# Window attention in a fused fp32 kernel: scores in 32-row tiles, keys staged per channel pair, TensorE's order skewed by one more unit

## The reference

```python
q = _win(roll(qs[idx], -4), 8)                      # 64 windows an image, 64 queries each
if idx == 0: k, v = _win(roll(ks[0])), _win(roll(vs[0]))     # 64 keys a window
else:        k, v = _win(roll(down(ks[1]))), _win(...)       # 2x2 stride-2 depthwise conv: 16 keys
atn = softmax(einsum('nqc,nkc->nqk', q, k) * SCALE, axis=-1)
y_  = einsum('nqk,nkc->nqc', atn, v)
```

## Time and profile before

| | |
|---|---|
| median of 3 runs | 864.39 us |
| profiled execution | 861.69 us |
| its span | 859.9 us |
| busy TensorE / VectorE / ScalarE / GpSimd | 692.2 / 719.1 / 584.7 / 603.3 us |
| mean granted TensorE clock | 0.964 |

### The profile page before, as it was taken

How to read it: one execution, slowest core, us unless ns; L and a number is a source line. 1 busy time by engine, 2 the same in 40 slices (tenths; PEclk the granted TensorE clock), 3 DMA queues, 4 the chain that set the end, 5 groups by cost and what they waited for, 6 DMA issues and landing times.

```text
span 859.9 us, 30275 instructions
## 1 busy us (share of the span) xinstructions
PE 692.2 (80%) x12282; PEld 500.2 (58%) x12282; DVE 719.1 (84%) x935; ACT 584.7 (68%) x1089; POOL 603.3 (70%) x401
## 2 busy tenths in 40 slices
PE   5968888885999958888888788888878887777763
PEld 1325565554446647666766666667666666555542
DVE  3469999997322119999999999999999999999975
ACT  2646776774213239788788798888888988777714
POOL 3047888781410008898898998999999999989960
PEclk9989999998999979999999999999999999999976
DMA  4000000000481148555555555565466555555302
GB/s 164 1 0 2 1 0 0 0 0 0 112 204 27 21 106 207 140 156 151 141 140 162 145 158 147 143 166 161 120 167 166 141 157 152 160 146 156 96 4 98
DMA packets 29937, 90.69 MB, mean 105 GB/s; under 512 B 10622, under 2 KB 10750, under 8 KB 29566
## 3 DMA queue, kind: packets, MB, share of 16 engines
q1 hardware_dynamic: 26672, 88.12, 38.3%
q10 hardware_dynamic: 3150, 0.88, 0.5%
HBM read 79.01 MB, written 3.28 MB: 96 GB/s over the span
## 4 chain that ended last, share of the span: by engine, by line
PE 40%; DVE 39%; issue 15%; ACT 2%; DMA 1%; POOL 1%; DVEq 1%; ACTq 0%; SPq 0%; POOLq 0%
PE PS L1128 40%; DVE region L767 19%; DVE region L779 9%; DVE region L645 2%; DVE region L601 2%; DVE region L605 1%; DVE region L620 1%; DVE region L607 1%; PE PS L1210 1%; DVE region L602 1%; DMA region<-px_scratch 1%; ACT region L874 0%; DVE region L575 0%; DVE region L561 0%; DMA cst<-in_consts 0%
## 5 line engine op out<-in xcount | busy, mean ns | idle before, releaser
L1128 PE MATMUL PS<-region 64*64 64x144 f32 (+3 forms) x10112 | 456.4, 292 | 112.6 <-issue 81.2
L1128 PEld LDWEIGHTS PS<-region 64*64 64x64 f32 (+1 forms) x10112 | 342.2, 134 | 219.9 <-issue 198.3
L767 DVE TENSOR_TENSOR region<-PS,region 128x864 f32<-128x864 f32 x384 | 381.2, 1046 | 12.4 <-PE PS L1128 12.3
L509 POOL TENSOR_TENSOR region<-region 128x768 f32<-128x768 f32 x128 | 202.4, 1581 | 67.5 <-DVE region L767 67.5
L513 POOL TENSOR_TENSOR region<-region 128x864 f32<-128x864 f32 x128 | 224.0, 1750 | 18.7 <-POOL region L509 0.4
L1006 ACT ACTIVATE region<-region 128x1152 f32<-128x1152 f32 x128 | 149.2, 1165 | 34.3 <-PE PS L1128 30.6
L1003 ACT ACTIVATE region<-region,cst 128x1152 f32<-128x1152 f32 x128 | 159.2, 1244 | 7.7 <-DMA region<-px_scratch 6.3
L779 DVE TENSOR_REDUCE region<-region 128x32 f32<-128x960 f32 x128 | 145.9, 1140 | 1.5 <-POOL region L513 1.5
L1037 ACT ACTIVATE region<-x,cst (+2 forms) x288 | 86.7, 414 | 0.0
L1128 PE MATMUL PS<-wg,xp 64*64 64x144 f32 x1024 | 82.6, 286 | 5.0 <-issue 4.9
L432 POOL TENSOR_TENSOR region<-region,cst 128x1024 f32<-128x1024 f32 x32 | 61.4, 1917 | 31.4 <-PE PS L1203 25.3
(11 more groups left out here) (118 smaller groups left out, 590.6 us busy)
## 6 DMA issues: line engine op xcount, KB each, us to landing
region<-px_scratch SPq DMA_DIRECT2D x256, 288.0 KB, 4.3
out<-region SPq DMA_DIRECT2D x4, 512.0 KB, 3.0
region<-xp SPq DMA_DIRECT2D x8, 140.2 KB, 2.9
region<-xp SPq DMA_DIRECT2D x8, 140.1 KB, 2.8
region<-xp SPq DMA_DIRECT2D x8, 140.0 KB, 2.9
cst<-in_consts SPq DMA_DIRECT2D x1, 1104.0 KB, 8.6
region<-xp SPq DMA_DIRECT2D x8, 132.0 KB, 2.7
region<-xp SPq DMA_DIRECT2D x8, 131.9 KB, 2.7
```

The lines of the kernel that those rows point to most:

```text
L509: pool.tensor_tensor(two_rows[:, :, :, 0:2 * THIRD - KEEP], two_rows[:, :, :, 0:2 * THIRD - KEEP], two_rows[:, :, :, KEEP:2 * THIRD], ALU. ...
L767: v.tensor_tensor(uu[:, 2 * u:2 * u + 2, :, THIRD * t:THIRD * (t + 1)], PS[:, 2 * t:2 * t + 2, 0:THIRD * C].rearrange("p h (a o) -> p h o ...
L1128: return nc.tensor.matmul(o, l, r, start=start, stop=stop)
```

## The change

- **Scores.** A product now takes 32 rows, the channels of two images (tile r, four of them), and 64 queries as weights, straight from `qw`. Its moving operand is `kb[part, i % 2, window]`: 160 columns, 64 + 64 keys of head 0 (each image of the pair masked by "e0") and 16 + 16 of head 1 ("e1"). Row tile r writes bank r, so the scores of one unit fill banks 0 to 3, and the outputs of attend move to bank 4, values and back to bank 5.
- **Staging.** ScalarE writes the masked keys, for a whole row of windows at once and one image of each pair at a time (`stage_keys`, two instructions of 512 and 128 elements, twice per row). GpSimd keeps one product per row: the halved values `vb` (1024 elements). `qs` and `vs` and their copies go away. The first keys are written between ScalarE's copies of the projections.
- **Values.** Head 0's values are picked by a product with every second group of 8 columns of the identity (four products 64x32), head 1's likewise (two products 128x64), where four transposes of 128x128 stood. ScalarE reads 64 + 128 columns of them. attend's products skip columns nobody reads (18 and 72 for 32 and 128).
- **Order.** attend and back come one unit later on TensorE, and VectorE inverts and normalises n-2 in unit n. back(n-3) also waits for `vt_out` of n-1, since it shares the bank.
- **Halving.** The last quarter (`halve(3)`) moves into units 4 to 7, one tap of both each.
- Loops are written out.

```diff
+            def stage_values(i):
+                pool.wait_ge(down_step, 8 * (i // 2 + 1))
+                if i >= 2:
+                    pool.wait_ge(vt_ready, done(4 * i - 5))
+                pool.tensor_tensor(
+                    vb[:, i % 2].rearrange("p w (b k) -> p w b k", b=B),
+                    kv4[:, WS * i:WS * (i + 1), 1, :].unsqueeze(2).to_broadcast([P, WS, B, K2]),
+                    mid(c_("h1"), WS).unsqueeze(3).to_broadcast([P, WS, B, K2]), ALU.mult).then_inc(vb_ready, 1)
+            stage_values(0)
+            for i in range(NWR):
+                if i < NWR - 1:
+                    stage_values(i + 1)
+                    pool.wait_ge(lead_step, 2 * i + 2)
+                    rows = x13[:, WS * (i + 1):WS * (i + 2), 1:W]
+                    pool.tensor_tensor(rows, rows, tap1, ALU.add).then_inc(lead_ready, 1)
...
-                    halve(n // 2 - 2)
-            halve(2)
-            halve(3)
+                    halve(n // 2 - 2, range(4))
+            halve(2, range(4))
...
-                s0 = PS[:, u, :].rearrange("p (b k) -> p b k", b=B)
-                s1 = PS[:, 2, 0:P].rearrange("p (b k) -> p b k", b=B)
+                s0 = PS[:, 0:4, 0:2 * K1].rearrange("p r (e k) -> p r e k", e=2)
+                s1 = PS[:, 0:4, 2 * K1:2 * (K1 + K2)].rearrange("p r (e k) -> p r e k", e=2)
+                top = sm[:, u, 0, :].rearrange("p (t r e) -> p t r e", t=2, e=2)
+                v.tensor_reduce(top[:, 0], s0, AX.X, ALU.max).then_inc(max_ready, 1)
+                v.tensor_reduce(top[:, 1], s1, AX.X, ALU.max).then_inc(max_ready, 1)
...
             def four_steps(i, parts):
                 for jj, which in enumerate(parts):
                     n = 4 * i + jj
-                    started = not (isinstance(n, int) and n == 0)
                     scores(n, jj % 2)
                     conv_taps(which[:-1], i)
-                    if started:
-                        invert(n - 1, (jj - 1) % 2)
+                    if n >= 2:
+                        invert(n - 2, jj % 2)
                     conv_taps(which[-1:], i)
-                    if started:
-                        normalise_heads(n - 1, (jj - 1) % 2)
+                    if n >= 2:
+                        normalise_heads(n - 2, jj % 2)
+                    if i == 1:
+                        halve(NCH // 2 - 1, (jj,))
             parts = (range(2, 4), range(4, 6), range(6, 8), range(8, 9))
             four_steps(0, (range(0, 3), range(3, 5), range(5, 7), range(7, 9)))
-            with dve.Fori(1, NWR - 1) as i:
+            for i in range(1, NWR):
                 four_steps(i, parts)
-            four_steps(NWR - 1, parts)
-            invert(31, 1)
-            normalise_heads(31, 1)
+            for n in (30, 31):
+                invert(n, n % 2)
+                normalise_heads(n, n % 2)
...
+            def stage_keys(i, e):
+                act.wait_ge(down_step, 8 * (i // 2 + 1))
+                if i >= 2:
+                    act.wait_ge(s_ready, done(4 * i - 5))
+                a.activation(kb[:, i % 2, :, K1 * e:K1 * (e + 1)], kw[:, i * CH:(i + 1) * CH].rearrange("p (w k) -> p w k", k=K1),
+                             ACT.Copy, scale=c_("e0")[:, e:e + 1]).then_inc(kb_ready, 1)
+                a.activation(kb[:, i % 2, :, 2 * K1 + K2 * e:2 * K1 + K2 * (e + 1)], kv4[:, WS * i:WS * (i + 1), 0, :],
+                             ACT.Copy, scale=c_("e1")[:, e:e + 1]).then_inc(kb_ready, 1)
+            by_rows(5)
+            stage_keys(0, 0)
+            by_rows(6)
+            stage_keys(0, 1)
+            by_rows(7)
...
-            def stage(n, u):
-                act.wait_ge(vt_ready, free(n))
-                act.sem_inc(act_turn, 1)
-                a.activation(qs[:, u], qw[:, bass.ds(n * 2 * K1, 2 * K1)].rearrange("p (w k) -> p w k", w=2), ACT.Copy).then_inc(q_staged, 1)
-                a.activation(vs[:, u], vw[:, bass.ds(n * 2 * K1, 2 * K1)].rearrange("p (w k) -> p w k", w=2).unsqueeze(2).to_broadcast([P, 2, 2, K1]),
-                             ACT.Copy).then_inc(q_staged, 1)
...
-            def four(i, last):
-                for jj in range(4):
-                    n = 4 * i + jj
-                    probs(n - 1, (jj - 1) % 2)
-                    values(n, jj % 2)
-                    if not last or jj < 3:
-                        stage(n + 1, (jj + 1) % 2)
-                    exps(n, jj % 2)
-                    if jj == 1:
-                        row_sum(i - 1)
-                    if jj == 0 and not last:
-                        lead(i + 1)
...
+            lead(1)
+            lead_left(1)
+            for n in range(36):
+                i, jj = n // 4, n % 4
+                if 1 <= n <= 32:
+                    exps(n - 1, (n - 1) % 2)
+                    values(n - 1, (n - 1) % 2)
+                if n >= 4:
+                    write(n - 4, WS * (i - 1) + SHIFT, 16 * jj + SHIFT)
+                if jj == 0 and 1 <= i < NWR - 1:
+                    lead_left(i + 1)
+                if jj == 0 and 1 <= i < NWR:
+                    row_sum(i - 1)
+                if jj in (1, 2) and i < NWR - 1:
+                    stage_keys(i + 1, jj - 1)
+                if jj == 3 and i < NWR - 2:
+                    lead(i + 2)
+                if 1 <= n <= 32:
                     probs(n - 1, (n - 1) % 2)
...
             def scores(n, u):
-                pe.wait_ge(staged, done(n, 2))
-                pe.wait_ge(q_staged, done(n, 2))
+                i, g = n // 4, 2 * (n % 4)
+                pe.wait_ge(kb_ready, 4 * (i + 1))
+                pe.wait_ge(q_out, done(i))
                 pe.wait_ge(sub_ready, 2 * n + 4)
+                for r in range(B // 2):
+                    part = slice(32 * r, 32 * (r + 1))
+                    for w in range(2):
+                        at = (2 * n + w) * K1
+                        ins = mm(PS[64 * w:64 * (w + 1), r, 0:2 * (K1 + K2)], qw[part, at:at + K1], kb[part, i % 2, g + w, :])
+                ins.then_inc(s_ready, 1)
+            def values(n, u):
+                i, g = n // 4, 2 * (n % 4)
+                pe.wait_ge(vt_out, 3 * n + 6)
+                pe.wait_ge(ye_out, n - 1 if n >= 4 else 0)
+                pe.wait_ge(vb_ready, i + 1)
+                pe.wait_ge(v_out, done(i))
+                head0 = ident.rearrange("p (t e c) -> p t e c", t=4, e=2)
                 for w in range(2):
-                    mm(PS[64 * w:64 * (w + 1), u, :], qs[:, u, w, :], kb[:, u, w, :])
-                    ins = mm(PS[64 * w:64 * (w + 1), 2, 0:P], qs[:, u, w, :], kvb[:, u, w, 0, :])
-                ins.then_inc(s_ready, 1)
-            def values(n, u):
-                pe.wait_ge(vt_out, 3 * n + 6)
+                    at = (2 * n + w) * K1
+                    for d in range(2):
+                        mm(PS[64 * d:64 * (d + 1), 5, 32 * w:32 * (w + 1)], vw[:, at:at + K1], head0[:, :, d, 0:CS])
                 for w in range(2):
-                    nc.tensor.transpose(PS[:, 4, w * P:(w + 1) * P], vs[:, u, w].rearrange("p d k -> p (d k)"), ident)
-                    ins = nc.tensor.transpose(PS[:, 4, 256 + w * P:256 + (w + 1) * P], kvb[:, u, w, 1, :], ident)
+                    ins = mm(PS[:, 5, 64 * (w + 1):64 * (w + 2)], vb[:, i % 2, g + w, :], ident.rearrange("p (b c) -> p b c", c=C)[:, :, CS:])
                 ins.then_inc(vt_ready, 1)
...
-                        mm(PS[part, 3, 32 * t:32 * (t + 1)], pts[:, u, t, part],
-                           v0[:, u, w, t].rearrange("p b c -> p (b c)"))
-                    ins = mm(PS[part, 3, P:2 * P], pts[:, u, 4, part], v1[:, u, w, :])
+                        mm(PS[part, 4, 32 * t:32 * (t + 1)].rearrange("p (b c) -> p b c", b=2)[:, :, 0:CS + 1], pts[:, u, t, part], v0[:, u, w, t, :, 0:CS + 1])
+                    ins = mm(PS[part, 4, P:2 * P].rearrange("p (b c) -> p b c", c=C)[:, :, CS - 1:], pts[:, u, 4, part],
+                             v1[:, u, w, :].rearrange("p (b c) -> p b c", c=C)[:, :, CS - 1:])
...
-                nc.tensor.transpose(PS[:, 5, 0:P], on[:, u, :], ident).then_inc(ot_ready, 1)
-            for n in range(4):
+                pe.wait_ge(vt_out, done(min(n + 2, 31), 3))
+                nc.tensor.transpose(PS[:, 5, 256:256 + P], on[:, u, :], ident).then_inc(ot_ready, 1)
+            for n in range(35):
+                if n < 32:
+                    scores(n, n % 2)
+                if 2 <= n <= 33:
+                    attend(n - 2, n % 2)
+                if 1 <= n <= 32:
                     probs(n - 1, (n - 1) % 2)
-                values(n, n % 2)
-                if n >= 2:
-                    back(n - 2, n % 2)
-                if n >= 1:
-                    attend(n - 1, (n - 1) % 2)
-            with pe.Fori(1, NWR) as i:
-                for jj in range(4):
-                    n = 4 * i + jj
-                    scores(n, jj % 2)
-                    probs(n - 1, (jj - 1) % 2)
-                    values(n, jj % 2)
-                    back(n - 2, jj % 2)
```

(15 more changed lines are left out.)

109 lines of the change are left out of this document (30 added, 79 removed).

## The result

The change makes the kernel slower: 899.56 us (median of 4 runs, 896.33 to 902.73) against 864.19 (4 runs, 861.30 to 865.27), a ratio of 1.0415 with the interval 1.0369 to 1.0460. The forecast was 846.5 in a range of 833 to 859. The profiled execution took 900.16 us with a span of 898.4 and a mean granted clock of 0.867; before it was 861.69, 859.9 and 0.964.

The account below looks back on a forecast made before the run. VectorE was taken to bound attention at 4.46 us a unit, and TensorE after the change. Period -14.2, start -6.6, halving +1.6 and end +1.3 sum to -17.9 us: 846.5 from 864.39, range 833 to 859.

Parts of the forecast that it names:

- Contention: Attention on VectorE: taps run about twice as long beside GpSimd; relieved, its unit falls from 4.46 to 3.58 us.
- Period at the full clock: Attention's time per unit: 4.0 us instead of 4.46 over 31 units, 14.2 us gained.
- TensorE's own sum: TensorE's attention unit: 3.19 us of instructions plus 0.85 for five changes of tile shape, 4.04 us.
- the forecast's loop through both engines: Attention: one TensorE unit, one VectorE unit and 0.3 us of semaphore steps make two periods, 3.96 us each.
- Scores: TensorE's 16 score instructions on 32-row tiles in a unit: 0.70 us, bounded by 0.65 and 0.82.
- Changes of shape: TensorE in attention: five changes of tile shape a unit at 0.17 us each, 0.85 us.
- The loads set the pace, so trimming saves nothing: TensorE's attend step: weight loads take 1.03 us for 20, so fewer columns save nothing, at best 0.2 us.
- Start: Beginning of attention: earlier keys let VectorE start near 55.6 us instead of 62.20, 6.6 us gained.
- End: Last units of attention: attend(30) stands before probs(31) and waits for normalise(29), 1.3 us lost.
- Rival 2: Attention on TensorE: shape changes cost 0.35 us each, unit 4.94 us, kernel 9.6 us slower at 874; chance 0.06.
- Rival 3: VectorE in attention: taps aren't slow because of GpSimd, unit stays 4.46 us, kernel 862.4 us; chance 0.03.
- rival 1: Attention: VectorE bounds at 3.58 us a unit, 29.3 us gained, kernel 835.1 us; chance 0.30.

Follow-up runs that it names:

- experiment 2: The changed kernel with five idle products in TensorE's first gap and one idle product of 512 columns in every unit: 852.81 us (7 runs).
- experiment 1: The changed kernel with five idle products bridging TensorE's first gap, behind values(0): 898.09 us (2 runs).
- experiments 3: The changed kernel with both trims undone, attend's products and head 0's values moving whole columns again: 856.54 us (1 run).
- experiment 5: The changed kernel with both trims undone and two idle products bridging TensorE's first gap: 848.69 us (4 runs).
- experiment 9: The changed kernel, all trims kept, with each scores product on all 128 rows instead of 32 (other numbers result): 844.02 us (1 run).
- experiment 4: The changed kernel with every scores product done twice, 16 more instructions a unit: 918.33 us (1 run).
- experiment 6: The changed kernel with trims undone, two bridging idle products, and probs(n-1) ahead of attend(n-2): 835.28, 910.63, 847.04 and 893.09 us.
- 11: The changed kernel with trims undone, first gap bridged, probs before attend, and an idle product of 192 columns in every unit: 843.68 us (4 runs).
- 7: The changed kernel with the trim undone for head 0's values only, attend still trimmed: 856.55 us (1 run).
- 8: The changed kernel with the trim undone for attend only, head 0's values still trimmed: 857.17 us (1 run).

## Why the prediction was wrong

**What failed: every duration of TensorE's unit was taken at the full clock, and no rival doubted it.** The sum 3.19 + 0.85 = 4.04 us was made from rows at a clock of 1.00 and answered "what does each instruction cost", but not "at which clock will a stage made of these run". Neither did the rivals. The clock stayed at half, and the unit was 5.66 us. A hint stood in the earlier trace rows: the first scores of the kernel before take 2.41 us for 8 instructions, at a clock of 0.50 to 0.58, and later ones, of which the forecast showed none, take 1.30:

```profile
74.81 1.30 PE L1128 MATMUL PS<-region 128*64 128x512 f32 x8 [0.35 <-DVE region L607]
```

What the runs show in its place is the same work at 1.2 GHz, 5.81 us a unit, which at 2.4 GHz TensorE would do in 3.32 (below). That the clock, and not the count of work, is what costs the time is shown by experiment 2, which adds work to the same products and is 45 us faster than experiment 1.

The terms, one by one:
- **Contention: right.** Taps beside an idle GpSimd take 0.69 to 0.73 us, all taps 739 ns in the mean instead of 1297, and a two-tap unit on VectorE of 3.48 us where the forecast had 3.49.
- **Period at the full clock: right in number, in part by luck.** 3.93 and 3.95 us (experiments 3 and 5) where 4.0 was forecast; experiment 9's 3.97 is a unit with dearer scores. Experiment 5's median of 848.69 lies 2.2 us over the forecast of 846.5, but between two pairs of executions, and that kernel moves the columns that the change had trimmed. Its gain over its own kernel before is 12.4, where 17.9 was forecast.
- **But TensorE's own sum was 0.72 us too high.** Experiment 2's unit of 4.38 us at full clock, less 1.06 for its extra product, is 3.32 with all gaps, against 4.04 (the terms of the first part add up to 3.18, not 3.19). Each with the changes of shape behind it, scores take 0.46 us instead of 0.87 and values 0.95 instead of 1.19. Untrimmed, the unit is 3.65 (111.77 to 115.42 in experiment 5), and the forecast's loop through both engines would give (3.65 + 3.58 + 0.3) / 2 = 3.77 where 3.95 was measured. That the loop sets the period there fits: neither engine is full (18.77 and 16.89 us of 20), and TensorE waits for VectorE in about half of the units:

```profile
108.61 1.25 PE L1109 MATMUL PS<-region 128*64 128x32 f32 x20 [0.85 <-DVE region L611]
```

  The two errors, a TensorE too slow and a loop too cheap, nearly cancel.
- **Scores: too dear.** 0.70 taken, 0.45 measured, the gap behind them included, below the lower bound of 0.65. Doubled scores (experiment 4) add 0.54 at half clock.
- **Changes of shape: right in size, too many.** The weight loader's gaps are 0.33 and 0.44 us at half clock, and 0.17 and 0.23 at full clock (experiment 1):

```profile
65.06 1.03 PEld L1109 LDWEIGHTS PS<-region 128*64 128x64 f32 x20 [0.23 <-issue]
...
66.87 0.88 PEld L1109 LDWEIGHTS PS<-cst,region 128*64 128x64 f32 x12 [0.17 <-issue]
```

  But only two of the five changes show one, before attend and before the values; before the probabilities and the next scores it is under 0.1 us at full clock. The Trainium skill (TensorEngine Tiling (Array Packing), Key Properties) says that a change of tiling mode drains the engine. The two gaps fit this rule, and they don't explain the loss.
- **"The loads set the pace, so trimming saves nothing": nearly right, and beside the point.** At full clock scores with attend take 1.57 us trimmed (experiment 1) and 1.66 whole (111.77 to 113.43 in experiment 5), so attend's trim saves the 0.1 that lies between the forecast's nothing and its 0.2 at best; head 0's saves 0.23 (0.94 against 1.17). But the columns weren't free to drop: with them the clock came back or stayed in most executions (not in two of experiment 6), with all trims, 32-row scores and no idle product in each unit it did in none of seven (mean clocks 0.862 to 0.876).
- **Start: near.** -4.95 us measured, -6.6 forecast. The first maximum is at 57.25 in the changed kernel and anywhere from 54.16 to 57.47 in the profiled experiments, whose code up to it is nearly the same, so that the difference is within what executions differ by.
- **End: right at full clock** (+1.5 in experiment 5, 1.3 forecast), +5.5 at half, since the chain of the last units is TensorE's as well. VectorE waits 4.02 and 3.50 us there:

```profile
239.62 0.26 DVE L604 RECIPROCAL region<-PS 128x16 f32<-128x16 f32 x1 [4.02 <-PE PS L1109]
...
243.76 0.26 DVE L604 RECIPROCAL region<-PS 128x16 f32<-128x16 f32 x1 [3.50 <-PE PS L1109]
```

Rival 2 had the right sign and TensorE as the bound, but its price, 0.35 us for each change of shape, was not the reason: at full clock its unit would be 3.6 to 3.8 us with the shape changes in it (an estimate: the loop with 3.32 for TensorE, (3.32 + 3.58 + 0.3) / 2 = 3.6, and experiment 5's 3.95 less half of the 0.33 that the trims save TensorE), and at half clock it is 5.8. Rival 3 fell with the taps; rival 1, VectorE as the bound at 3.58, came nowhere: experiment 6 is near its period, 3.78 in its profiled execution, but with TensorE as the bound. Shown over several executions is that the stage runs at half clock because of what TensorE is given in it: an idle product in every unit lifts it (experiment 2, and 11 against 6). That the rows of the scores (experiment 9 against the change) and the trimmed columns (experiments 3, 7 and 8) each decide whether it comes back rests on one execution each. Not shown is what exactly the chip watches; row tiles put alone into the kernel before, and the new order alone, were not tried. How often versions 5 and 11 would lose the clock over many more executions is open as well.

## What to carry to other kernels

Cost a change to TensorE's tiles at both clock levels, and read the granted clock of that stage first in the trace after it: row tiles saved TensorE about 0.6 us of a unit here and trims 0.3, and together they cost the clock, about 2 us a unit. Whole columns, or a small idle product in every unit, can be the cheaper form: with whole columns, a bridge and 0.43 us of idle product a unit took 4.17 us instead of 5.66. Look at several executions before trusting such a version, since one may keep the clock where the next loses it.

## What was not expected of the hardware

- TensorE ran at half clock for some 198 us (about 59 to 257), 181 of them without a wait, and the clock rose only after the stage had ended. In one execution of a stage with the same instructions, but 128-row scores, it came back within a unit after each of two falls.
- One idle product of 192 columns in a unit of 4.17 us kept the clock high over the whole stage (four executions, and ten with 384 columns); the same program without it took anything from 835.28 to 910.63 us in four.
- Doubling the 32-row products (16 more instructions per unit) changed nothing in the clock (one execution).
- Sixteen instructions of 160 columns on 32-row tiles take 0.45 us where the same on 128 rows take about 1.1: row tiles do run beside each other (the idle product of 192 columns takes 0.43 us for two instructions, by which 16 of 160 columns one after another would take 2.9 us, an estimate), and are the quicker form for these scores as long as the clock holds.
